# Reordering the gather of a graph network step on VectorE and ScalarE, and its degree stage, on one Trainium2 core

## The reference, cut to what matters

```python
xn = _layernorm(x)
# graph convolution
deg  = segment_sum(ew_sl, row_sl, N)              # by source, self-loops with weight 1
dinv = where(deg > 0, rsqrt(deg), 0)
msgs = (xn @ W)[col_sl] * (dinv[row_sl] * ew_sl * dinv[col_sl])[:, None]
h7   = segment_sum(msgs, row_sl, N) + b
gcn  = relu(h7 @ W1 + b1) @ W2 + b2
# attention: k and v are normalised per head of 32, kv = k^T v / N, out = q kv
mix  = gelu((q @ kv + xn) @ w1 + b1) @ w2 + b2 + xn
x    = x + gcn + mix
x    = x + ffn(_layernorm(x))                     # 8 experts, the best 2 of each node
```

## Time and profile before

| | us |
|---|---|
| median of 3 runs (range) | 4517.35 (4515.73 to 4520.52) |
| the profiled execution | 4502.67 |
| its span | 4500.9 |
| busy in the span: TensorE, VectorE, GpSimd, ScalarE | 3399.5, 2931.0, 2770.0, 1429.0 |
| joined stage | 802.7 to 1018.9 |
| gathers of the gather stage, first start to last start | 1020.6 to 3509.3 |
| last add of the gather stage ends | 3529 |

### The profile page before, as it was taken

One profiled execution on the slowest core, in us unless ns is written; L12 is line 12 of the kernel. 1 busy time (PEld: TensorE's weight loads), 2 busy tenths in 40 slices (PEclk: granted clock), 3 DMA queues, 4 the chain that ended last, 5 costly groups with the idle time before them and its releaser, 6 DMA issues. The chain is left out here.

```text
span 4500.9 us, 75623 instructions
## 1 busy us (share of the span) xinstructions
PE 3399.5 (76%) x20283; PEld 2597.3 (58%) x20283; DVE 2931.0 (65%) x7496; ACT 1429.0 (32%) x4439; POOL 2770.0 (62%) x2543
## 2 busy tenths in 40 slices
PE   7677777246777777777756777777777589999995
PEld 6455554243444444444435666566665479999885
DVE  8899998674565565655655555555555665555676
ACT  2455554440111111111002222222322255555442
POOL 0488888436666666666666666666666245555553
PEclk9678787557888888888868888888888799999998
DMA  2111111763333333333334444444446612222466
GB/s 76 17 3 3 3 3 3 239 228 116 110 108 111 110 112 108 111 110 111 109 89 119 128 131 131 130 130 132 128 130 121 139 46 70 68 70 68 148 217 215
DMA packets 285822, 472.50 MB, mean 105 GB/s; under 512 B 95011, under 2 KB 180778, under 8 KB 285743
## 3 DMA queue, kind: packets, MB, share of 16 engines
q0 software_dynamic: 140544, 273.69, 24.5%
q1 hardware_dynamic: 138047, 193.90, 12.7%
q10 hardware_dynamic: 7154, 3.99, 0.3%
HBM read 350.11 MB, written 123.70 MB: 105 GB/s over the span
## 5 line engine op out<-in xcount | busy, mean ns | idle before, releaser
L1621 POOL DMA_INDIRECT rows<-table,idx x1664 | 1675.1, 1007 | 815.5 <-issue 497.3
L1904 DVE TENSOR_TENSOR acc<-acc,ps_seg 128x256 f32 x1664 | 695.5, 418 | 955.5 <-remote 761.6
L2069 PE MATMUL ps_seg<-rows,pick 128*128 128x256 f32 x3328 | 997.3, 429 | 272.0 <-DVE acc L1904 182.0
L2069 PEld LDWEIGHTS ps_seg<-rows,pick 128*128 128x128 f32 x3328 | 660.4, 213 | 514.0 <-issue 404.6
L771 POOL DMA_INDIRECT records<-sort_rec,sort_addr x280 | 528.8, 1889 | 260.7 <-DVE sort_rec L874 158.7
L1746 DVE TENSOR_SCALAR pick<-iota_row,loc,ewt 128x128 f32<-128x128 f32 x1680 | 529.2, 363 | 5.6 <-remote 1.8
L2509 POOL DMA_INDIRECT y_rows<-arena,idx x212 | 249.8, 1178 | 290.0 <-DVE arena L2556 185.2
L2641 PE MATMUL ps_h<-arena,up_now 128*128 128x128 f32 x3392 | 417.8, 277 | 0.0
L2625 PE MATMUL ps_y<-down_now,arena 128*128 128x256 f32 x1696 | 401.4, 380 | 0.0
L2641 PEld LDWEIGHTS ps_h<-arena,up_now 128*128 128x128 f32 x3392 | 398.3, 193 | 1.9
L926 PE MATMUL ps_out<-acc 128*128 128x240 bf16 x1568 | 281.5, 364 | 142.0 <-DVE acc L860 141.9
(11 more groups left out here) (385 smaller groups left out, 5122.7 us busy)
## 6 DMA issues: line engine op xcount, KB each, us to landing
rows<-table,idx POOLq DMA_INDIRECT x1664
acc<-y_rows SPq DMA_DIRECT2D x28, 640.0 KB
xn<-xn_dram SPq DMA_DIRECT2D x100, 128.0 KB
table<-acc SPq DMA_DIRECT2D x98, 128.0 KB
xT_dram<-xT SPq DMA_DIRECT2D x98, 128.0 KB
xn<-xT_dram SPq DMA_DIRECT2D x49, 256.0 KB
skip<-skip_dram SPq DMA_DIRECT2D x49, 256.0 KB
x_rows<-acc SPq DMA_DIRECT2D x49, 256.0 KB
```

The lines of the kernel that those rows point to most:

```text
L1621: pool.indirect_dma_start(out=rows[:, t, :], out_offset=None, in_=k.table, in_offset=bass.IndirectOffsetOnAxis(idx[:, h, t:t + 1], 0), bou ...
L1904: dve.tensor_tensor(here, here, sums(u), ALU.add).then_inc(added[u], 1)
L2069: last = pe.matmul(sums(t), pick[:, h, t, :], rows[:, t, :], start=True, stop=True)
```

## The change

In the gather stage:
- VectorE alternates one pick, one add, and waits for a pair of sums after the first of its picks (before: two picks, the wait, two adds).
- The mask `rsv` of the last block's missing nodes is no operation of its own; the scaling of k and v (`scaled`) multiplies by it as a scalar.
- The normalising of a pair for the FFN moves from VectorE to ScalarE (two ACTIVATEs with scale rstd and bias shift), behind `aggregated` and ahead of `features`; VectorE computes shift = −mean × rstd on 128x2.
- Places in the block are unpacked for all 1664 tiles at once behind the first 16 picks (`locate`); weights are read from the records in place. In a step `unpack` makes only `idx`, and each pick takes its scalars at a place computed from the loop's register.
- `places` is kept as two rows, on partitions 0 and 32, so the setup loads it with two transfers.
- `t1`, `t2`, `t3` and `kvT` of the fold share memory with `xT`, and the fold waits for the transfers out of it.

In the joined stage: LEAD is 3 (was 5), moments and deviations run two chunks ahead, inverses one; ScalarE scales before it normalises; it scales all blocks of a group but for half of the last group; from group 8 on it issues the stores of its own blocks. A new operation on GpSimd (`spread`) writes the partition's number where a record's weight is 0, and VectorE takes the maximum with word 0, so that empty records point to 128 rows instead of one.

```diff
-    LEAD = 5
+    LEAD = 3
+    ACT_STORES = 8
-        act_share = lambda j: range(READY[j], READY[j] + len(ready(j)) * 3 // 4)
+        act_share = lambda j: range(READY[j], READY[j] + (len(ready(j)) if j + 1 < TRIPS else len(ready(j)) // 2))
                     if b.stop > numbers_from:
-                        sp.wait_ge(two_done, 2)
+                        sp.wait_ge(spread_done, 2)
                 def put_table(j):
+                    by_sp = ready(j) if j < ACT_STORES else dve_share(j)
...
+                def spread():
+                    pool.wait_ge(unturned, len(turns))
+                    pool.wait_ge(two_done, 2)
+                    pool.wait_ge(const_done, 2)
+                    pool.tensor_scalar(high_i, k.recs[:, 0:TILES, 1], 0.0, tile_col[:, 0:1], ALU.is_equal, ALU.mult).then_inc(spread_done, 1)
...
+                    if j >= ACT_STORES:
+                        at = k.naturals(act, READY[j], len(act_share(j)))
+                        act.wait_ge(act_scaled, act_total(j))
+                        for u, n in enumerate(act_share(j)):
+                            act.dma_start(table_blocks[:, bass.ds(at[u], 1), :], k.acc[:, n:n + 1, :]).then_inc(table_out, 16)
                 for g in range(GROUPS_T + 6):
                     c = g + LEAD
-                    if c + 1 < NORMS:
-                        moments(c + 1)
+                    if c + 2 < NORMS:
+                        moments(c + 2)
                     if g < GROUPS_T:
                         one_hots(g)
+                    if g == 1:
+                        dve.wait_ge(spread_done, 1)
+                        dve.tensor_tensor(k.recs[:, 0:TILES, 0], k.recs[:, 0:TILES, 0], high_i, ALU.max).then_inc(spread_done, 1)
...
+                def normalised(i):
+                    start_after(act, rows_out, 16 * i)
+                    start_after(act, f_done, i)
+                    act.wait_ge(shift_done, i + 1)
+                    act.sem_inc(head_held, 1)
+                    for h in both:
+                        act.activation(xl[:, h:h + 1, :], k.acc[:, bass.ds(2 * i + h, 1), :], ACT.Identity,
+                                       scale=rstd[:, h:h + 1], bias=shift[:, h:h + 1]).then_inc(xl_done, 1)
...
                         if due(i):
                             aggregated(n, i)
                         if due(i - 2):
+                            normalised(i - 2)
                             features(i - 2)
...
+                def make_pick(h, n, t):
+                    at = bass.ds(n * STEP_TILES + t, 1)
+                    made = dve.tensor_scalar(pick[:, h, t, :], k.iota_row[:, :], loc[:, at], ew[:, at],
                                              ALU.is_equal, ALU.mult)
...
+                    dve.scalar_tensor_tensor(
+                        out=kv_heads(u), in0=by_head4(raw[:, u, :]), scalar=k.valid[:, bass.ds(m, 1)],
+                        in1=rs[:, :].rearrange("p (c h) -> p c h", c=2 * DC).unsqueeze(3).to_broadcast(
+                            [P, 2 * DC, HEADS_PER_CHUNK, HEADC]), op0=ALU.mult, op1=ALU.mult).then_inc(k_scaled, 1)
...
                     unpack(1 - h, n + 1)
-                    dve.wait_ge(loc_done, n + 2)
                     for t in range(STEP_TILES):
-                        make_pick(1 - h, t)
                         half, at = t // SLOT, t % SLOT
+                        make_pick(1 - h, n + 1, t)
+                        if t % 2 == 0:
+                            dve.wait_ge(summed_up[t // 2], n + 1)
+                        if t > 0:
+                            dve.wait_ge(added[t - 1], n + 1)
+                        else:
+                            start_after(dve, added[ALL_TILES], n)
+                        here = acc_row[:, bass.ds(places[t], D)]
+                        dve.tensor_tensor(here, here, sums(t), ALU.add).then_inc(added[t], 1)
                         if t % 2 == 0:
                             continue
```

More of the change, by code:

```diff
@@ L373, in _ @@
                 sp.wait_ge(places_out, 16)
-                sp.dma_start(k.places[:, :], k.places_dram.rearrange("(o b) t -> o (b t)", o=1)).then_inc(places_in, 16)
-                sp.wait_ge(places_in, 16)
+                for h in range(2):
+                    sp.dma_start(k.places[h * (P // 4):h * (P // 4) + 1, :].rearrange("o (b t) -> o b t", t=STEP_TILES),
+                                 k.places_dram.rearrange("(b h) t -> h b t", h=2)[h:h + 1, :, :]).then_inc(places_in, 16)
+                sp.wait_ge(places_in, 32)
                 sp.wait_ge(place_in, 16)
@@ L960, in degrees_rows_table @@
     READY = [BLOCKS * P * j // TILES_USED for j in range(TRIPS)] + [BLOCKS]
-    assert TRIPS * P == TILES and HALF_BANK * WIDE <= 512 and HEAD + 2 < LEAD and LEAD + 3 < NORMS <= GROUPS_T + LEAD
+    assert TRIPS * P == TILES and HALF_BANK * WIDE <= 512 and HEAD + 1 == LEAD and LEAD + 3 < NORMS <= GROUPS_T + LEAD
     assert all(READY[j + 1] <= NORM * (2 * j + 2 + LEAD) for j in range(TRIPS))
@@ L1075, in put_table @@
                 def put_table(j):
-                    at = k.naturals(sp, READY[j], len(ready(j)))
+                    by_sp = ready(j) if j < ACT_STORES else dve_share(j)
+                    if not by_sp:
+                        return
+                    at = k.naturals(sp, by_sp.start, len(by_sp))
                     sp.wait_ge(act_scaled, act_total(j))
                     sp.wait_ge(dve_scaled, dve_total(j))
-                    for u, n in enumerate(ready(j)):
+                    for u, n in enumerate(by_sp):
                         sp.dma_start(table_blocks[:, bass.ds(at[u], 1), :], k.acc[:, n:n + 1, :]).then_inc(table_out, 16)
@@ L1165, in _ @@
                 piece(0, ew)
-                deviations(HEAD)
+                normalised(HEAD)
                 act.wait_ge(rest_done, 2)
                 piece(1, rest)
-                normalised(HEAD)
+                deviations(LEAD)
                 act.wait_ge(rest_done, 4)
                 piece(2, rest2)
-                for c in range(HEAD + 1, LEAD):
-                    deviations(c)
-                    normalised(c)
-                deviations(LEAD)
+                deviations(LEAD + 1)
                 def keep_sums(j):
@@ L1247, in _ @@
                 inverses(1)
-                for c in range(HEAD, LEAD):
-                    moments(c)
+                moments(HEAD)
+                inverses(HEAD)
                 for n, g in enumerate(range(0, TRIPS, 4)):
@@ L1274, in _ @@
                 rests(0, ew, rest)
-                inverses(HEAD)
+                moments(LEAD)
                 rests(1, rest, rest2)
-                moments(LEAD)
-                for c in range(HEAD + 1, LEAD):
-                    inverses(c)
+                moments(LEAD + 1)
+                inverses(LEAD)
                 dve.wait_ge(two_done, 2)
@@ L1449, in gather_and_mix @@
         rstd = sb("rstd3", [P, 2])
+        shift = sb("shift3", [P, 2])
         wr = sb("wr", [P, DC, N_EXPERTS])
@@ L1786, in from_sums @@
                     dve.wait_ge(k_all_summed, 1)
+                    for q in range(LOOKAHEAD):
+                        dve.wait_ge(xT_out[q], 16 * (FULL + (LEFT + q < BLOCKS)))
                     dve.tensor_scalar(t1[:, :, :], VK, hg, None, ALU.mult).then_inc(kv_step, 1)
@@ L1843, in inverse @@
                     dve.wait_ge(std_done, i + 1)
+                    start_after(dve, xl_done, 2 * i)
                     dve.reciprocal(rstd[:, :], std[:, :]).then_inc(rstd_done, 1)
-                def normalised(i):
-                    start_after(dve, rows_out, 16 * i)
-                    start_after(dve, f_done, i)
                     dve.wait_ge(rstd_done, i + 1)
                     dve.sem_inc(head_held, 1)
-                    for h in both:
-                        dve.tensor_scalar(xl[:, h:h + 1, :], k.acc[:, bass.ds(2 * i + h, 1), :], mv[:, h, 0:1],
-                                          rstd[:, h:h + 1], ALU.subtract, ALU.mult).then_inc(xl_done, 1)
+                    dve.scalar_tensor_tensor(out=shift[:, :], in0=mv[:, :, 0], scalar=-1.0, in1=rstd[:, :],
+                                             op0=ALU.mult, op1=ALU.mult).then_inc(shift_done, 1)
                 def scores(i):
@@ L1885, in step @@
                         return
-                    places = places_of(n)
+                    places = places_of(n, h)
                     start_after(dve, summed_up[SLOT - 1], n)
                     unpack(1 - h, n + 1)
-                    dve.wait_ge(loc_done, n + 2)
                     for t in range(STEP_TILES):
-                        make_pick(1 - h, t)
                         half, at = t // SLOT, t % SLOT
+                        make_pick(1 - h, n + 1, t)
[7 more added lines that the diff above has]
+                        dve.tensor_tensor(here, here, sums(t), ALU.add).then_inc(added[t], 1)
                         if t % 2 == 0:
                             continue
```

(9 more changed lines are left out.)

77 lines of the change are left out of this document (34 added, 43 removed).

## The result

The changed kernel takes 4531.67 us (median of 8 runs, 4526.96 to 4536.1), the kernel before 4515.61 us beside it: a ratio of 1.0036, with a 95% interval of 1.0027 to 1.0046. It is 16 us slower. The time lies in the forecast range, but the sign is that of rival A. The profiled execution of the changed kernel has a span of 4529.8 us.

What follows compares the result with a forecast made beforehand. The gather stage was taken as bound by 1.30 us a gather plus stalls on late signals, not VectorE's work. −15 + 5 − 3 + 1 − 12 = −24 us gave 4493 us; own range 4470 to 4508, 8-in-10 range 4440 to 4540.

Steps and rivals of the forecast that it cites:

- rival A: Pair steps: the 1.0 us delay reaches GpSimd whole, VectorE's relief worth nothing; +48, −12, −15 for others, 4538 us; chance 0.22.
- steps with k and v: Gather stage, with plain steps: fewer VectorE operations and picks between adds, less register operations: −15 us, ends +7 and −60.
- pair steps: Gather steps that finish a pair of blocks: half-hidden delay +24, VectorE's relief −19, together +5 us, ends −19 and +48.
- joined stage: Stage before the gathers: shorter prelude, scalings moved to ScalarE, stores issued by two engines: −12 us, ends −20 and 0.
- one-time costs: Unpacking all places at once behind the first 16 picks +1 us (0 to 4); second transfer of places +0 to 1.
- The bound of the stage: Gather stage: 1.00 us a gather plus 0.30 issue, 1.30 us at best, 2163 us in all; stalls come on top.
- rival C: Gather stage: VectorE sets the stalls, so a third of GpSimd's remote waits goes, −97 us; 4432 us in all; chance 0.10.
- The price of VectorE's work: Gather steps: 0.15 us of step per microsecond of VectorE, from steps with k and v against plain ones; upper reading.
- relief terms: VectorE's removed work at 0.15: −17 us over 51 steps with k and v or plain, −19 over 48 pair steps.
- register operations: Picks at computed addresses, 16 per step: between nothing and 24 us, taken as near nothing; sign: idle issue gaps before picks.
- pair chain: Pair steps: normalising on ScalarE starts the transposes 1.0 us later in 48 steps; +48 us unhidden, +24 with half hidden.
- The gather's end: Last 52 tiles, all empty records: spread over 128 rows they land sooner, −3 us (0 to −10).

Runs made afterwards that it cites:

- before_again: The kernel before, unchanged, run and profiled again on a chip with stalls: ratio 0.9992, span 4481.5 us.
- after_again: The changed kernel, unchanged, run and profiled again on the chip with stalls: ratio 1.0036 to the kernel before, span 4497.9 us.
- picks_paired: The changed kernel with VectorE's old order (two picks, the wait, two adds), on a chip with stalls: ratio 1.0036 to the kernel before.
- unpack_each: The changed kernel with places unpacked in every step again and the picks' scalars at fixed addresses, on a chip with stalls: ratio 0.9985 to the kernel before.
- no_spread: The changed kernel without the two operations that spread the empty records over 128 table rows, on a chip with stalls: ratio 1.0038 to the kernel before.
- joined_only_2: The kernel before with the changed kernel's joined stage: ratio 0.9964 on a chip with stalls; as joined_only, on one without, 0.9912.
- norm_dve: The changed kernel with the pair's normalising back on VectorE behind the reciprocal: ratio 0.9936 to the kernel before without stalls, 0.9993 with stalls.
- regs_kept: The changed kernel with places unpacked step by step into the large buffer, picks still at computed addresses: ratio 0.9938 to the kernel before, without stalls, twice.

## Why the prediction was wrong, point by point

Term by term, forecast against before_again and after_again: steps with k and v −15 and +9.0, pair steps +5 and +20.0, end −3 and −8.1, joined stage −12 and −4.3, one-time costs, fold and plain steps +1 and +2.3. The −2.5 us behind the stage had no term.

- **The bound of the stage** was right: 1.30 us a gather, plus stalls. On chips without stalls the stage runs at 1.31. That VectorE's order does not set the stalls was right too: rival C is refuted by picks_paired.
- **The price of VectorE's work, 0.15 us a microsecond,** was the first wrong step. It came from a comparison of two phases that differ in TensorE's work also, and I said so, but then used it for both kinds of steps. picks_paired, for the order of picks and adds, gives 1.9 us a step of relief for 0 us. The masks and the unpackings have no clean run of their own (unpack_each puts 0.66 us of operations back and is faster, but takes the register operations away as well), but no kind of step became shorter with all of the relief in place. So the relief terms (−17, −19) are what no run bears out. One of them was also read too large: the scaling that carries the mask takes 0.743 us and not 0.684, which takes back 0.12 of the 0.57 us a step.
- **The register operations and the unpacking once** were the second, and the larger. I bounded the register operations at 24 us and took "near nothing, because VectorE's queue is idle before half of the adds"; I priced the unpacking at +1 us, and its two large operations indeed take only 1.17 and 1.03 us behind the first picks. Together they cost 23 us. How, stays open, as said above. My reading is that an engine's idle share says nothing about a delay that sits between a late signal and the next signal sent on; no run isolates this.
- **The pair chain** was right in mechanism and size: 1.06 us later, +24 us forecast with half of it hidden, 19 us measured. This is rival A's own term, which took the whole 48 us. Rival A's total, 4538, is near the measured 4531.67 by luck: it says that the relief is worth nothing and still keeps −15 us for "all other terms", most of which is relief. Without it the same sum gives 48 − 12 − 3 + 1 = +34 us, twice the loss.
- **The gather's end:** −3 forecast, −8.1 us in the two profiles side by side, −3.3 in the first two, and some 23 us on chips without stalls. The range ended at −10. I read one late pair of rows in one timeline and not the queue behind it.
- **The joined stage:** −12 forecast, −4.3. The tail did shrink. The end of the stage in after_again:

```profile
1005.46 1.71 ACT L1203 ACTIVATE acc<-acc,dinv 128x256 f32<-128x256 f32 x4 [0.57 <-DVE dinv L1347]
...
1007.32 1.95 ACTq L1208 DMA_DIRECT2D table<-acc  x4
1007.32 1.91 SPq L1086 DMA_DIRECT2D table<-acc  x4
1013.01 0.20 POOL L1622 MEMSET headmask<- 128x128 f32 x1 [30.43 <-POOLq L122]
```

  The next stage starts 5.8 us behind the last scaling's end, where it was 18.2 us (1000.7 by the earlier trace rows to 1018.9). But the last scaling ends at 1007.2, not at 1000.7: the last two groups follow one another by 7.6 us on ScalarE (997.83 and 1005.46), as ScalarE now scales and issues, and the spread's 5 us come on top. I had the 7.3 us a group and charged only 2 us in all for it, and had no price for the spread on GpSimd. In no_spread the last scaling ends at 1002.3 and the first gather starts 9.2 us earlier than in before_again, so the term without a price is most of what is missing from the −12.

With the measured terms the sum is: pair chain +19, unpacking once +23, joined stage −4, end −8, which is +30, against +16 measured. By the ratios the gap is smaller: the gather edits cost 0.0072 (32 us) over joined_only_2, and the two parts 42 us. Either the other gather edits give some 10 us, of which no run shows a sign, or the two costs are not separate and undoing either gives part of the other back; 10 us are hardly more than the noise of such a difference, and no run settles it.

## What to carry to other kernels

Before you price relief of an engine, find out whether that engine's work ends the waits: here it was busy for 1436 of the stage's 2532 us and 1.9 us a step less between its adds were worth nothing, while a delay of 1 us in its chain to other engines cost 19 us, and unpacking once with computed addresses, which takes operations away from it, cost 23. Padding records should not all point at one row. And time a change on more than one chip: this one is 0.36% slower on chips with stalls, while its nearest variants on the others (norm_dve, regs_kept) are 0.6% faster than the kernel before; the changed kernel itself was not run there.

## What was unexpected of the hardware

The kernel before takes 4209 to 4220 us (medians) in three sets of runs and 4486 to 4516 us in three others on other chips. The whole difference lies in the gather stage: from first to last gather joined_only takes 2174.9 us and joined_only_2, the same kernel, 2468.1, where the spans are 4190.9 and 4467.1. On the slower kind 5.0 us pass in the median from TensorE's sum to VectorE's add (before_again), on the other 0.24 (joined_only), and the mean granted clock of the executions is 0.84 to 0.85 against 0.88 to 0.90. A GpSimd operation on 128x1664 integers took 6.0 us, the same on VectorE 1.08. Gathers of 128 times the same row land late when many follow one another: their packets take 0.51 us against 0.14, and without stalls 26.0 us pass from the last gather to the last matmul, against 3.3 us when the rows differ.
